# First pass of a graph attention: scores turned ten pairs ahead in every chunk, score copies and releases moved from 22 to 25 pairs ahead

## The reference, cut to what matters

```python
scores = einsum('ehd,hd->eh', h_src, attn_src) + einsum('ehd,hd->eh', h_dst, attn_dst)
scores = where(scores > 0, scores, 0.2 * scores)
amax = maximum(segment_max(scores, dst), 0.0)
w = exp(scores - amax[dst])
w = w / (segment_sum(w, dst) + 1e-12)[dst]
out = segment_sum(h_src * w[..., None], dst)
```

## Time and profile before

| | |
|---|---|
| median of 3 runs | 2853.38 us (2851.15 to 2854.49) |
| the profiled execution | 2854.25 us |
| its span, first to last instruction | 2852.4 us |
| the stage: first gather of it to its last sum | 359.4 to 860.6 us |
| mean granted clock of TensorE | 0.891 |
| in the stage: gathers (L1459) | 362 x 953 ns, 344.8 us busy |
| in the stage: pair products (L1539) | 880 x 448 ns, 269.1 us busy |
| in the stage: weighing (L1695), adding (L1709) | 220 x 698 ns, 220 x 425 ns |
| in the stage: one-hots (L1549, L1552) | 440 x 387 ns, 44 x 1362 ns |

### The profile page before, as it was taken

How to read it: one execution, slowest core, us unless ns; L and a number is a source line. 1 busy time by engine, 2 the same in 40 slices (tenths; PEclk the granted TensorE clock), 3 DMA queues, 4 the chain that set the end, 5 groups by cost and what they waited for, 6 DMA issues and landing times. The chain is left out here.

```text
span 2852.4 us, 42642 instructions
## 1 busy us (share of the span) xinstructions
PE 2291.0 (80%) x11329; PEld 1711.2 (60%) x11329; DVE 1313.4 (46%) x3497; ACT 1076.8 (38%) x2885; POOL 1377.5 (48%) x1407
## 2 busy tenths in 40 slices
PE   6899847767677988999997787877754888875798
PEld 5455535445455877888886465554543777764577
DVE  6553456766676130111114232242248666655851
ACT  3323544545441211333333443265420665542221
POOL 0122477777730051212211677767767777775300
PEclk9999867888788899999998898888775999998899
DMA  3466544444411025777774433344557444443201
GB/s 98 153 219 220 181 110 122 119 120 118 119 50 41 10 95 152 196 221 205 210 211 130 141 106 106 106 122 124 162 147 236 125 132 134 131 123 116 95 12 33
DMA packets 249527, 374.45 MB, mean 131 GB/s; under 512 B 66472, under 2 KB 186740, under 8 KB 249322
## 3 DMA queue, kind: packets, MB, share of 16 engines
q0 software_dynamic: 70000, 179.80, 22.8%
q1 hardware_dynamic: 132740, 140.88, 16.1%
q10 hardware_dynamic: 46582, 51.38, 5.5%
HBM read 298.68 MB, written 73.27 MB: 130 GB/s over the span
## 5 line engine op out<-in xcount | busy, mean ns | idle before, releaser
L2724 POOL DMA_INDIRECT cm_rows<-rows,e_bsrc x392 | 373.3, 952 | 179.0 <-issue 101.2
L1181 POOL DMA_INDIRECT store<-rows,e_bsrc x392 | 377.3, 963 | 119.5 <-issue 107.3
L1459 POOL DMA_INDIRECT at_rows<-values,e_brow x362 | 344.8, 953 | 115.1 <-issue 90.5
L2861 PE MATMUL cm_part<-cm_rows,cm_one 128*128 x880 | 268.0, 447 | 89.8 <-SPq L2737 62.8
L1539 PE MATMUL at_part<-at_msg,store 128*128 128x265 f32 x880 | 269.1, 448 | 86.8 <-DVE at_msg L1695 42.7
L1206 PE MATMUL banks<-ag_msg,ag_one 128*128 128x258 f32 x880 | 228.0, 397 | 70.3 <-issue 45.7
L2861 PEld LDWEIGHTS cm_part<-cm_rows,cm_one 128*128 128x128 f32 x880 | 181.7, 220 | 158.7 <-issue 134.9
L1539 PEld LDWEIGHTS at_part<-at_msg,store 128*128 128x128 f32 x880 | 175.8, 218 | 156.7 <-DVE at_msg L1695 66.7
L2161 POOL DMA_INDIRECT x_sum<-x_y,x_target x56 | 87.1, 1555 | 340.7 <-DVE x_y L2274 333.3
L3077 DVE TENSOR_TENSOR store<-store,cm_part 128x256 f32 x220 | 92.2, 419 | 339.1 <-PE cm_part L2861 311.1
L1206 PEld LDWEIGHTS banks<-ag_msg,ag_one 128*128 128x128 f32 x880 | 165.4, 195 | 117.2 <-issue 57.3
(11 more groups left out here) (685 smaller groups left out, 3920.2 us busy)
## 6 DMA issues: line engine op xcount, KB each, us to landing
x_w<-in_L_ffn_W1p SPq DMA_DIRECT2D x32, 1024.0 KB, 5.2
x_w<-in_L_ffn_W2p SPq DMA_DIRECT2D x32, 1024.0 KB, 5.5
values<-at_rows ACTq DMA_DIRECT2D x25, 1088.0 KB, 6.0
p_brow<-local_row SPq DMA_DIRECT2D x44, 320.0 KB, 4.0
xn_acc<-low_row SPq DMA_DIRECT2D x28, 448.0 KB
expert_in<-store POOLq DMA_DIRECT2D x7, 1040.0 KB, 8.1
at_rows<-values,e_brow POOLq DMA_INDIRECT x392, 2.8
cm_rows<-rows,e_bsrc POOLq DMA_INDIRECT x392, 2.7
```

The lines of the kernel that those rows point to most:

```text
L1181: pool.indirect_dma_start(rows[:, b % slots, k, :], None, table, bass.IndirectOffsetOnAxis(index[:, k, b:b + 1], 0)).then_inc(gathered[b % ...
L1459: pool.indirect_dma_start(rows[:, b % RING, k, :], None, table, bass.IndirectOffsetOnAxis(e.block_row[:, k, b:b + 1], 0)).then_inc(gathere ...
L2724: pool.indirect_dma_start(rows[:, b % SLOTS, k, :], None, table, bass.IndirectOffsetOnAxis(e.block_src[:, k, b:b + 1], 0)).then_inc(gather ...
L2861: last = pe.matmul(part[:, n % deep, :], one[:, n // U % 2, k, u, :], rows[:, bass.ds(at[u] % SLOTS, 1), k, :].squeeze(1), start=(k == 0), ...
```

## The change

In every chunk but the first, PE's and ScalarE's steps take the places that only the last chunk had: PE at lo-10, -7, -6, -5, -4 and -2, ScalarE at lo-9, lo-3 and lo. ScalarE's steps stand at the head of their pair, ahead of that pair's one-hots and copies, for all pairs after 0. FREE grows from 22 to 25, for the score copies from pair 0 on and for SP's releases from the first block on. The copies ahead of pair 0 stay as they were, so at pair 0 four copies are made at once. DVE's places, the ring of 28 and the instructions themselves stay.

```diff
-RING, FREE = 28, CH + LEAD
+RING, FREE = 28, CH + LEAD + 3
...
-    pe_steps, act_steps = ({n: step for n, step in step_of.items() if step[1] != last_at} for _ in range(2))
-    pe_steps.update({last_at + d: (len(CHUNKS) - 1, *CHUNKS[-1], i) for i, d in enumerate((-10, -7, -6, -5, -4, -2))})
-    act_steps.update({last_at + d: (len(CHUNKS) - 1, *CHUNKS[-1], i) for i, d in ((0, -9), (3, -3), (6, 0))})
+    pe_steps, act_steps = ({n: step for n, step in step_of.items() if step[0] == 0} for _ in range(2))
+    for pc, (lo, m) in enumerate(CHUNKS[1:], 1):
+        pe_steps.update({lo + d: (pc, lo, m, i) for i, d in enumerate((-10, -7, -6, -5, -4, -2))})
+        act_steps.update({lo + d: (pc, lo, m, i) for i, d in ((0, -9), (3, -3), (6, 0))})
+    soon = [min(G, n + 1 + (FREE if n >= 0 else CH + LEAD)) for n in range(-LEAD, G)]
     hurry = G - 5 * U
...
-            for n in range(FREE - LEAD):
+            for n in range(CH):
                 fetch(n)
+            have = CH
             for n in range(-LEAD, G):
                 if n == hurry:
-                    for late in range(n + FREE, G):
+                    for late in range(have, G):
                         fetch(late)
-                if n > hurry and n in act_steps:
+                    have = G
+                if n > 0 and n in act_steps:
                     softmax(*act_steps[n])
                 if n >= 0 and n % U == 0 and n + U < G:
                     hots(n // U + 1)
-                if n < hurry:
-                    fetch(n + FREE)
+                for late in range(have, soon[n + LEAD]):
+                    fetch(late)
+                have = max(have, soon[n + LEAD])
                 if n > 0 and n % 8 == 0 and n // 8 + 1 < NT:
                     take(n // 8 + 1)
-                if n <= hurry and n in act_steps:
+                if n <= 0 and n in act_steps:
                     softmax(*act_steps[n])
```

More of the change, by code:

```diff
@@ L1413, in attend @@
     last_at = CHUNKS[-1][0]
-    pe_steps, act_steps = ({n: step for n, step in step_of.items() if step[1] != last_at} for _ in range(2))
-    pe_steps.update({last_at + d: (len(CHUNKS) - 1, *CHUNKS[-1], i) for i, d in enumerate((-10, -7, -6, -5, -4, -2))})
-    act_steps.update({last_at + d: (len(CHUNKS) - 1, *CHUNKS[-1], i) for i, d in ((0, -9), (3, -3), (6, 0))})
+    pe_steps, act_steps = ({n: step for n, step in step_of.items() if step[0] == 0} for _ in range(2))
[3 more added lines that the diff above has]
+    soon = [min(G, n + 1 + (FREE if n >= 0 else CH + LEAD)) for n in range(-LEAD, G)]
     hurry = G - 5 * U
-    assert hurry % U == 0 and hurry + FREE < G
+    assert hurry % U == 0
     with Mem(nc) as m_, stage(nc, "cleared", "ready", "freed", "apart", "hot", "weighted", "multiplied", "summed",
```

## The result

The changed kernel takes 2915.41 us (median, 2909.48 to 2919.25) against 2853.79 before (2851.15 to 2854.49): a ratio of 1.0215, interval 1.02 to 1.0231. It is slower by 62 us, where 49 were forecast.

What follows compares the result with a forecast made beforehand. The gather and pair work, nearly equal per chunk, bound the stage. Five chunks at 32.0 us plus 16.5, 7.0 and 12.4 made 195.9; turn 13 came 49 us later, giving 2903 us, range 2850 to 2935.

Steps and rivals of the forecast that it cites:

- What bounds the kernel: Graph attention's first pass: POOL's gathers set a floor of 35.8 us per 16-pair chunk; pair work takes about as long, 35.4.
- Turn to pair lo: PE, from a chunk's turn to its first pair (lo): 23.6 us in a regular chunk, before added delays.
- slow clock: PE after long waits at the turn: slow turn and next two pairs, 7.0 us per five chunks, some 17 in all.
- residue: A chunk's first pair number modulo 5; one-hots are made for five pairs at a time, so it decides what meets what.
- The template: Last chunk of the kernel before, lo = 208, already with the new offsets: pair lo 22.5 us after its turn.
- Pair lo to the next turn: PE, six pairs and a second token product from a chunk's first pair on: 8.4 us per chunk, without waits at the turn.
- The waits at the turn: PE waiting for ScalarE's copy of the chunk's last scores, behind one-hots: 16.5 us per five chunks, against 12.9 before.
- The fade of residue 2: ScalarE's fade at lo, behind one-hots at lo-2, comes 3.1 us after pair lo; cost taken as 0.9 us.
- The exponential: ScalarE's step at lo-3, behind earlier one-hots: delays PE's back-turn 6.2 us for residue 4, 2.0 us for residue 0.
- The sum: Five chunks take 195.9 us against 177.1 before; turn 13 comes 49 us later, with 37.4 us behind it.
- SP's release: SP's slot release moved from 22 to 25 blocks behind its position: cost taken as zero, upper bound 4 us per chunk.
- A: Rival: pairs get as fast as the gather, nothing is lost, only the tail gains: 2851 us; chance 0.20.

Runs made afterwards that it cites:

- the spread steps: Changed kernel with PE's steps 2 to 5 one pair later (lo-5, -4, -3, -1), nothing else: 2855.15 us, ratio 1.0008.
- order and reach: Changed kernel with every PE and ScalarE step back at lo-6+i; copies and releases 25 ahead and ScalarE's steps at the pair's head kept: 2854.95 us, ratio 1.0019.
- the last one: Changed kernel with copies 28 ahead, exponential at lo-5, fade at lo-2, PE's steps 2 to 5 one pair later, SP's releases at 22: 2842.36 us, ratio 0.9964.
- the three edits: Changed kernel, one edit each: copies 28 ahead, 2861.38 us; exponential at lo-5 and fade at lo-2, 2887.35 us; PE's steps 2 to 5 one pair later, 2855.15 us.
- the run with 22: Changed kernel with only SP's release put back to 22 blocks behind its position: 2913.4 us, ratio 1.0215.

## Why the prediction was right, and by how much it was short

The stated range reached down to 2850 us, where nothing is lost, so the measured time lying in it says little by itself. What the runs test is the forecast of 2903 us and the mechanism behind it.

**What bounds the kernel.** Right. Three changed kernels as different as the spread steps, order and reach, and the last one all start their last gather between 811.9 and 813.5 us, as before. Gains below 35.8 us per chunk vanish: the three edits give back 54, 28 and 60 us by themselves, 142 together, of 62 that were lost.

**Turn to pair lo**, the term that was too small. By the sum's terms (23.6, slow clock, exponential) and as measured in the first and the second five chunks:

| residue | forecast, us | measured, us |
|---|---|---|
| 1 | 23.6 + 2.8 = 26.4 | 27.9, 26.4 |
| 2 | 23.6 + 1.4 = 25.0 | 27.6, 27.1 |
| 3 | 23.6 | 24.5, 24.0 |
| 4 | 23.6 + 6.2 = 29.8 | 31.9, 32.1 |
| 0 | 23.6 + 2.8 + 2.0 = 28.4 | 28.4, 27.9 |
| sum | 133.2 | 140.3, 137.5 |

Two sizes in it were off. The template is the last chunk, which has 12 instead of 16 pairs, with products of 96 instead of 128 (rows of L1504 to L1517 in the earlier trace rows); its first step comes 5.8 us after the turn, in chunk 4 after the change 6.6 (526.11 - 519.54). And for residue 2 I took half of the slow clock. Its turn waits 3.62 us in chunks 2, 7 and 12; in chunk 2 it is slow itself (1.19 us, second row of the turns), in chunk 7 it is not, but the three pairs behind it take 4.37 us where those of chunk 4 take 2.85:

```profile
647.27 0.68 PE L1491 MATMUL at_turn<-ident,at_src 128*128 128x128 f32 x4 [3.62 <-ACT at_src L1573]
...
648.73 4.37 PE L1541 MATMUL at_part<-at_msg,store 128*128 128x265 f32 x12
```

```profile
520.84 2.85 PE L1541 MATMUL at_part<-at_msg,store 128*128 128x265 f32 x12
```

**Pair lo to the next turn.** 62.7 us for five chunks by the terms (five times 8.4, waits 16.5, fade 4.2); measured 63.4. The sum is right, two of its parts are not, and that they cancel is luck: from pair lo to the next turn it is 13.2 us in chunk 1 where the terms give 14.6, and 12.5 in chunk 2 where they give 11.2. The waits at the turn were forecast at 5.9, 4.9, 2.9, 1.9 and 0.9 us for residues 0 to 4; the rows show 5.95, 5.73, 3.62, none and 1.58. The fade of residue 2 was taken at 0.9 us. In chunk 12, on ScalarE and then PE:

```profile
872.04 1.36 ACT L1554 ACTIVATE store<-store,ones 128x1280 f32<-128x1280 f32 x1
...
874.89 0.17 ACT L1589 ACTIVATE at_fade<-at_small 128x8 f32<-128x8 f32 x1
```

```profile
877.97 2.11 PE L1541 MATMUL at_part<-at_msg,store 128*128 128x265 f32 x4 [3.25 <-DVE at_msg L1700]
```

The fade comes 3.0 us after pair lo (871.9), as forecast (3.1), but PE then stands 3.25 us and the pair behind is slow (2.11 us). The delay was right and its price was not: the first sum of a chunk waits for the fade, and the pairs behind it for that sum.

**The exponential.** Right in place: chunks 4 and 9 are the ones, behind the one-hots at lo-4. The back-turn was forecast at +22.3 us and is at +23.7 (543.27 - 519.54), 1.4 us later; PE's step 3 ahead of it is 1.2 us behind the template (534.74 - 519.54 = 15.2 against 14.0).

**The sum.** Turn 13 was forecast 49 us late and is 61.3: 7.8 us are missing in the first five chunks (203.7 against 195.9), 2.4 in the second (198.3), 1.4 in chunks 11 and 12 (78.6 against 77.2), 0.6 in the first turn. The tail was the template's, as said.

**The slow clock.** It was priced at some 17 us of the sum. Two comparisons over the whole stage bear on it, both with the same 1262 instructions on PE: against the kernel before PE is busy 10.8 us longer, against the run with copies 28 ahead, whose turns hardly wait, 23.1 us. The 17 us lie between the two. The Trainium skill, "TensorE: Matmul & The Clock Gate", Part 1, gives the ramp's penalty, for modeling, as under 1% of a typical kernel span. For what this stage shows, 23.1 of 2907.6 us or 0.8%, the figure holds. It is no reason to drop the term here, since the change itself lost only some 2%.

**SP's release** was taken at zero, and the run with 22 shows no difference. Gathers were to end near 860 us, with long waits on the release, and end at 860.2 with waits up to 6.9.

**The rivals.** A, pairs as fast as the gather, failed for this kernel and came true with PE's steps one pair further apart: 2855 us. Its condition (35.8 us per chunk) was the right one; what missed it were the places of the steps, and copies 28 ahead alone come within 0.3% of before. The Trainium skill, "Perfetto Trace Analysis", section "Optimization Strategy", asks for dependencies that start sooner or complete faster: here the sooner start with the steps one pair apart lost 62 us, and the same start with room between them lost nothing that can be told (1.0008).

**What the prediction did not see.** It added the holds as if each were independent. The spread steps show that they hang together: the pairs held by PE delay DVE's sums, with its next step behind them, and the one-hots, with the exponential and the copies behind those. And it took the reach for free, whereas reach without the new order costs some 22 us; why is not shown.

## What to carry to other kernels

In a queue that runs in order, a chain between engines needs as much ready work between two of its steps as the other engine takes to answer; an earlier start with the steps close together holds ready work behind every step, and the other engine's answer can then stand behind that very work. A step put ahead of its own pair's bulk work still stands behind the bulk work of earlier pairs, so its place has to be chosen against those. Find the floor first (here the gather, 35.8 us per chunk): below it edits gave nothing but a shorter tail, and gains found one by one did not add up.

## What the runs showed of the hardware that was not expected

Executions of one kernel on the same chip lie up to 20 us apart (the kernel before between 2838.52 and 2858.29 in 21 runs), so a tenth of a per cent takes many of them. The rest of the program, which the change leaves alone, was 6.0 us shorter in one profiled execution than in the other. Where ScalarE loads five block numbers into registers behind one-hots, it is idle for 1.14 and 1.15 us (rows of L1572 at 593.20 and L1573 at 542.70 above), where 0.84 was taken from the start of the stage.
